# Moving half of the probability transposes that TensorE did to the DMA engines, in a two-head attention loop on one core

## The reference

```
x: (2, 1024, 256)
c_kv = x @ w_dkv                  # rank 64, shared by all heads
c_q  = x @ w_dq                   # rank 192
q, k = heads of c_q, c_kv         # 64 rotary + 128 plain columns each
attn = softmax(q k^T / sqrt(192)) # per head: 1024 queries x 1024 keys
out  = attn v;  y = out @ w_o
x = layernorm(x + y)
x = layernorm(x + (silu(x w1q^T) * (x w3q^T)) w2q^T)
```

## Time and profile before

| | |
|---|---|
| median of three runs | 1011.03 us (1008.86 to 1012.56) |
| the profiled execution | 1020.05 us, of which its span 1017.9 us |
| mean granted clock of TensorE | 0.981 of full speed |
| TensorE busy | 965.2 us, 95% of the span |
| VectorE, ScalarE, GpSimd busy | 741.0, 603.5, 605.3 us |
| one pair of heads, steady | 43.42 us for 16 tiles |

### The profile page before, as it was taken

One profiled execution on the slowest core, in us unless ns is written; L12 is line 12 of the kernel. 1 busy time (PEld: TensorE's weight loads), 2 busy tenths in 40 slices (PEclk: granted clock), 3 DMA queues, 4 the chain that ended last, 5 costly groups with the idle time before them and its releaser, 6 DMA issues.

```text
span 1017.9 us, 18739 instructions
## 1 busy us (share of the span) xinstructions
PE 965.2 (95%) x5622; PEld 696.4 (68%) x5622; DVE 741.0 (73%) x1164; ACT 603.5 (59%) x1036; POOL 605.3 (59%) x643
## 2 busy tenths in 40 slices
PE   7989999999999999998979989999999999997985
PEld 3548766766676766667866866766666676675874
DVE  1756788888888888863456678888888888885455
ACT  2636777777767666751333587766766766764132
POOL 0007777777777777760340787777777777674034
PEclk9799999999999999999989999999999999999998
DMA  9553755545454544566100575655545455457101
GB/s 260 148 217 88 143 103 101 94 95 103 93 96 93 106 94 96 100 140 261 44 23 22 120 129 94 102 100 99 96 89 103 93 97 99 94 103 190 59 1 42
DMA packets 288450, 107.62 MB, mean 106 GB/s; under 512 B 274492, under 2 KB 282512, under 8 KB 287376
## 3 DMA queue, kind: packets, MB, share of 16 engines
q1 hardware_dynamic: 286944, 97.03, 46.1%
q10 hardware_dynamic: 880, 7.86, 2.1%
q0 software_dynamic: 576, 2.10, 0.6%
HBM read 23.85 MB, written 7.60 MB: 31 GB/s over the span
## 4 chain that ended last, share of the span: by engine, by line
PE 73%; issue 10%; DVE 8%; POOL 4%; ACT 2%; DMA 2%; SPq 1%; ACTq 0%; POOLq 0%; DVEq 0%
PE Sa L1045 17%; PE Sb L1045 15%; PE Oa L1072 15%; PE Tb L1054 5%; PE Ta L1054 4%; DVE nmax L753 4%; PE Sb L1096 2%; DVE Q_lo L767 2%; PE Sa L1096 2%; POOL g_lo L415 1%; PE Ob L1082 1%; PE Sb L1172 1%; DMA xr<-in_L_attn_x_dram 1%; POOL P_parts L383 1%; PE Sa L1015 1%
## 5 line engine op out<-in xcount | busy, mean ns | idle before, releaser
L753 DVE TENSOR_REDUCE nmax<-Sa 128x1 f32<-128x1024 f32 x128 | 155.9, 1218 | 78.5 <-PE Sa L1045 77.1
L383 POOL TENSOR_TENSOR P_parts<-probs_a,P_parts 128x512 f16<-128x512 f32 x128 | 169.6, 1325 | 23.5 <-POOL P_parts L380 23.5
L753 DVE TENSOR_REDUCE nmax<-Sb 128x1 f32<-128x1024 f32 x128 | 156.0, 1219 | 20.0 <-PE Sb L1045 20.0
L383 POOL TENSOR_TENSOR P_parts<-probs_b,P_parts 128x512 f16<-128x512 f32 x128 | 149.2, 1166 | 23.9 <-POOL P_parts L380 23.9
L439 ACT ACTIVATE PT_hi<-Ta 128x512 f16<-128x512 f32 x128 | 76.3, 596 | 110.6 <-PE Ta L1054 110.6
L380 POOL TENSOR_SCALAR P_parts<-probs_a 128x512 f16<-128x512 f32 x128 | 80.8, 631 | 75.8 <-ACT probs_a L538 70.4
L380 POOL TENSOR_SCALAR P_parts<-probs_b 128x512 f16<-128x512 f32 x128 | 80.9, 632 | 51.1 <-ACT probs_b L538 48.9
L351 POOL TENSOR_TENSOR turned<-qmul 128x1024 f32<-128x1024 f32 x16 | 38.1, 2404 | 112.2 <-DVE qmul L748 112.2
L1045 PE MATMUL Sb<-K_hi,Q_hi 128*128 128x512 f32 x256 | 91.0, 436 | 7.8 <-ACT probs_b L538 4.0
L1045 PE MATMUL Sa<-K_hi,Q_hi 128*128 128x512 f32 x256 | 93.0, 444 | 0.0
L538 ACT ACTIVATE probs_b<-Sb,nmax 128x1024 f32<-128x1024 f32 x64 | 71.4, 1116 | 33.0 <-DVE nmax L756 33.0
(11 more groups left out here) (298 smaller groups left out, 2118.6 us busy)
## 6 DMA issues: line engine op xcount, KB each, us to landing
QO<-turned SPq DMA_DIRECT2D x64, 128.0 KB, 2.3
TT<-ternary SPq DMA_DIRECT2D x2, 2304.0 KB, 11.5
PT_dma<-P_parts SPq DMA_TRANSPOSE x256, 3.0
ternary<-tern ACTq DMA_DIRECT2D x1, 2304.0 KB, 8.2
wo<-in_L_attn_w_o_dram SPq DMA_DIRECT2D x4, 512.0 KB, 8.1
xq<-in_L_attn_x_dram SPq DMA_DIRECT2D x2, 1024.0 KB, 9.7
wq_high<-Wq_hi ACTq DMA_DIRECT2D x1, 2048.0 KB, 12.7
Wvo_lo<-wvo_low ACTq DMA_DIRECT2D x2, 1024.0 KB, 5.7
```

The costliest lines, as they stand in the source:

```text
L383: nc.gpsimd.tensor_tensor(P_parts[:, n % DEEP, 1, :], src, P_parts[:, n % DEEP, 0, :], ALU.subtract).then_inc(part_lo, 1)
L753: nc.vector.tensor_reduce(nmax[:, n % 4:n % 4 + 1], SS[n % 2][:, :], AX.X, ALU.max, negate=True).then_inc(row_max, 1)
```

## The change

Six of the eight key blocks are turned by DMA in place of four, TensorE turns two. The cast of the high part for DMA goes from GpSimd to ScalarE; GpSimd keeps the subtraction. ScalarE and VectorE evict the turned blocks of two tiles at once, at odd n. The values are multiplied four key blocks at a time, at n = 3, 7, 11 and 15. P_parts grows by half, so a part of Wq_lo is saved to DRAM and read back for the second sequence; buffers in the shared area move.

```diff
-KD = KT // 2
+KP = 2
+KD = KT - KP
+SPILL = 4
...
                 if b + 1 < B:
...
-                    sp.wait_ge(wq_out, 16)
+                    sp.wait_ge(wq_out, 32)
                     sp.dma_start(Wq_hi[...], wq_high).then_inc(wq_in, 16)
+                    sp.dma_start(Wq_lo[:, 0:SPILL]..., wq_low).then_inc(wq_in, 16)
...
# GpSimd
-                    hold(pool, exp_done, EXP0 + tile + 1)
-                    if reused is not None:
-                        hold(pool, part_in[n % DEEP], reused)
-                    nc.gpsimd.tensor_scalar(P_parts[:, n % DEEP, 0, :], src, 1.0, 1.0, ALU.mult,
-                                            ALU.mult).then_inc(part_hi, 1)
                     hold(pool, part_hi, tile + 1)
-                    nc.gpsimd.tensor_tensor(P_parts[:, n % DEEP, 1, :], src, P_parts[:, n % DEEP, 0, :],
+                    nc.gpsimd.tensor_tensor(P_parts[:, n % DEEP, 1, :], probs[n % DEEP][:, KP * P:S],
+                                            P_parts[:, n % DEEP, 0, :], ALU.subtract).then_inc(part_lo, 1)
...
# ScalarE, before the loop over the sequences
             act_.wait_ge(prod_hi, PAIRS)
             act_.wait_ge(qr_hi, 4)
+            act_.wait_ge(prod_lo, PAIRS)
+            act_.wait_ge(qr_lo, 4)
+            act_.dma_start(wq_low, Wq_lo[:, 0:SPILL]...).then_inc(wq_out, 16)
...
+                def part_high(tile, n, reused):
+                    act_.wait_ge(exp_done, EXP0 + tile + 1)
+                    if reused is not None:
+                        act_.wait_ge(part_in[n % DEEP], reused)
+                    copy(P_parts[:, n % DEEP, 0, :], probs[n % DEEP][:, KP * P:S]).then_inc(part_hi, 1)
...
# ScalarE, in iteration n, behind the exponent of tile n+1
-                        if first and n == 1:
-                            act_.wait_ge(wq_out, 16)
+                        if first and n == 0:
+                            act_.wait_ge(wq_out, 32)
+                            act_.wait_ge(rope_sum, b * 2 * GROUPS + 2 * GROUPS)
...
-                        transposed_high(t0 + n, n)
+                        part_high(t0 + n, n, None if first and n < DEEP else 16 * (t0 // DEEP + n // DEEP))
+                        if n % 2:
+                            transposed_high(t0 + n, n)
...
# VectorE, in iteration n, behind the maximum of tile n+2
-                        transposed_low(t0 + n, n)
+                        if n % 2:
+                            transposed_low(pair * (TILES // 2) + n // 2, n)
...
# TensorE
-                    for k in range(KD):
+                    for k in range(KP):
...
-                            if n % 2 == 1:
-                                for k in range(n % 8 - 1, n % 8 + 1):
+                            if n % 4 == 3:
+                                for k in range(n % 8 - 3, n % 8 + 1):
                                     values(pair * 2 + n // 8 - 1, 1 - n // 8, k)
```

More of the change, by code:

```diff
@@ L62, in build @@
     wq_high = nc.dram_tensor("wq_high", [P, H * 2 * P], F, kind="Internal").ap()
+    wq_low = nc.dram_tensor("wq_low", [P, SPILL * 2 * P], F, kind="Internal").ap()
     wvo_low = nc.dram_tensor("wvo_low", [P, PAIRS * D], F, kind="Internal").ap()
@@ L116, in build @@
         (TT,), _ = lay(HEAD_AT, ("TT", [P, W], R))
-        (PT_hi, PT_lo, PT_dma), _ = lay(
-            SHARED_AT, ("PT_hi", [P, 2, 2, KD, HALF], F16), ("PT_lo", [P, 2, 2, KD, HALF], F16),
-            ("PT_dma", [P, 2, 2, 2 * KD, HALF], F16))
+        (PT_dma, PT_hi, PT_lo), _ = lay(
+            SHARED_AT, ("PT_dma", [P, 2, 2, 2 * KD, HALF], F16), ("PT_hi", [P, 2, 2, KP, HALF], F16),
+            ("PT_lo", [P, 2, 2, KP, HALF], F16))
+        PT_END = SHARED_AT + 2 * 2 * 2 * KD * HALF * 2
         (xq, xT, tcos, tsin, wkr, wkv, wdq, wdq_b), WORK_AT = lay(
@@ L132, in build @@
         (turned,), _ = lay(SHARED_AT, ("turned", [P, 2, S], F))
-        PT_BYTES = KT * S * 2
         (res1,), AT = lay(WORK_AT, ("res1", [P, 4, D], F))
-        assert AT <= SHARED_AT + 2 * PT_BYTES
-        (xr, res0, x1a), _ = lay(
-            SHARED_AT + 3 * PT_BYTES, ("xr", [P, QT, D], F), ("res0", [P, 4, D], F), ("x1a", [P, 4, D], F))
+        assert PT_END - 24 * S <= WORK_AT and AT <= PT_END - 16 * S
+        (res0, xr, x1a), AT = lay(
+            PT_END - 16 * S, ("res0", [P, 4, D], F), ("xr", [P, QT, D], F), ("x1a", [P, 4, D], F))
+        assert AT <= PT_END
         (x1b, x1T_hi0, x1T_lo0), AT = lay(
-            SHARED_AT + 2 * PT_BYTES, ("x1b", [P, 4, D], F), ("x1T_hi0", [P, KC, HALF], R),
-            ("x1T_lo0", [P, KC, HALF], R))
-        assert AT <= SHARED_AT + 3 * PT_BYTES
+            PT_END, ("x1b", [P, 4, D], F), ("x1T_hi0", [P, KC, HALF], R), ("x1T_lo0", [P, KC, HALF], R))
+        assert AT <= SHARED_AT + 64 * S
         def tok(halves, t):
@@ L289, in _ @@
                 if b:
-                    sp.wait_ge(wq_in, 16)
+                    sp.wait_ge(wq_in, 32)
                     sp.sem_inc(wq_ready, 1)
@@ L389, in pair_pool @@
                         h = n // 8
-                        split_probs(pair * TILES + n, n,
-                                    None if first and n < DEEP else 16 * (pair * TILES // DEEP + n // DEEP))
+                        low_probs(pair * TILES + n, n)
                         if n % 8 == 0 and not (first and h == 0):
@@ L1047, in scores, with transpose_probs @@
                     last.then_inc(scores_ready, 1)
-                def transpose_probs(tile, n, waited):
+                def transpose_probs(tile, tile2, n, waited):
                     if not waited:
                         pe.wait_ge(exp_done, EXP0 + tile + 1)
-                    pe.wait_ge(pt_lo, tile + 1)
-                    for k in range(KD):
-                        last = nc.tensor.transpose(TS[n % 2][:, k * P:(k + 1) * P],
+                    if n % 2 == 0:
+                        pe.wait_ge(pt_lo, tile2 + 1)
+                    for k in range(KP):
+                        at = (n % 2 * KP + k) * P
+                        last = nc.tensor.transpose(TS[n // 2 % 2][:, at:at + P],
                                                    probs[n % DEEP][:, k * P:(k + 1) * P], ident[:, :])
@@ L1133, in pair_pe @@
                             scores(t0 + n + 2, (n + 2) % TILES, pair + (n + 2) // TILES)
-                        transpose_probs(t0 + n, n, not (last and n >= TILES - 2))
+                        transpose_probs(t0 + n, pair * (TILES // 2) + n // 2, n, not (last and n >= TILES - 2))
                         if first and n == 8:
```

38 lines of the change are left out of this document (20 added, 18 removed).

## The result

The changed kernel takes 1059.59 us (median of four runs, 1058.29 to 1063.81), the kernel before 1011.79 (four runs, one more than the three behind 1011.03): a ratio of 1.0476, with a 95% interval of 1.0426 to 1.0526. Slower, as forecast, inside the range of 1020 to 1068, and 17 us above the 1043 that was named. The two profiled executions are 1058.37 and 1020.05 us, 38 us apart, the medians 48: the profiled execution of before was some 9 us above its own median, that of after was not.

The account below looks back on a forecast made before the run. PE bounds the kernel, 5.27 us per two tiles, just above a 4.40 us loop of scores, maximum and exponent. Terms of 16.1 us a sequence, twice, plus 0.4, say 32, added to the median 1011.03 gave 1043; range 1020 to 1068.

Parts of the forecast that it names:

- The turn and the cycle: Attention loop: scores, maximum, exponent, next scores into the same banks take at least 4.40 us; four tiles take 11.24 us.
- S4: Third scores after a block of values: wait for an exponent, cannot start before 4.40 us after the first scores.
- S5: Fourth scores after a block of values: start at 6.71 us, not 6.03, since cast and eviction delay their exponent on ACT.
- the block of 24: The 24 value matmuls on PE after every fourth tile: 2.72 us.
- the cast's hold: Time the new 768 column cast holds ACT's queue ahead of an exponent: 0.72 us, between 0.49 and 0.95.
- the 13 us more: Whole time added if the cast on ACT cost the skill's 0.94 us, holding ACT 0.22 us longer.
- the rest of a pair: Beyond four cycles of 11.24 us, the Q_lo split at n = 12 delays an exponent some 0.2 us: pair 45.2 us.
- The ends: Outside the steady pairs, per sequence: tiles without values 0.5 + 0.4 us more, last pair 1.2, tail up to xr 2.7.
- (a): Rival: PE is the only bound, 1.2 us per four tiles come out, 70 us off, 941 us; chance 0.04.
- (b): Rival: the cast hardly holds ACT, cycle 10.56 us, 1003 us; chance 0.09, including a cast near its lower bound.
- (c): Rival: DMA sets the pace, ACT waits at its cast for landings; 400 us more, milder case 1100; chance 0.05.
- (d): Rival: PE's clock falls because PE waits more; 1057 us if tiles without values ran at half clock; chance 0.06.

Follow-up runs that it names:

- the last one: Changed kernel with values two key blocks at a time, both casts behind the next even tile's exponent, Q_lo splits at n = 11 and 15: 994.50 us, ratio 0.9758.

## Why the prediction was right, and where its sum was off

**The turn and the cycle.** Right, with its mechanism, and to the hundredth: 11.24 us predicted, 11.25 measured. S4 at 4.43 (4.40 predicted), S5 at 6.74 (6.71), the block of 24 at 2.71 (2.72), the cast's hold at 0.73 (0.72). The gaps on PE are those foretold, 0.91 ahead of S4 and 0.41 ahead of S5. ACT's busy time is the one sign that was off: 36.8 us of a pair, not 39, since I had added recorded times, which overlap. With the cast out of the way the cycle is the 10.56 that the prediction named. The Trainium skill (ScalarE: Activation LUTs, Rules for kernel authors) gives the 0.94 us for an ACTIVATE whose bias is a pointer operand, which this cast does not have; the trace shows a recorded 0.84 and a hold of 0.73, so the 13 us more did not come. For an operation that follows another one of ACT the distance between starts is the price. The 0.72 was a halfway guess between two rows; the copies of 512, 768 and 1024 columns hold ACT for 0.48, 0.73 and 0.95 us, so the guess was near because the price goes nearly with the columns.

**Which of the two matters more.** The grouping by four. The prediction said that gathering the blocks leaves one of two turns bare and eats the whole saving on PE; the run with nothing but the grouping shows 2.6 us a pair lost where PE's work is unchanged. The cast's place adds 0.7 in a cycle without other waits, and 0.9 in a pair as it stands.

**The step that was mis-sized: the rest of a pair.** The prediction charged DVE's queue with 0.2 us a pair ("the Q_lo split at n = 12 now comes between maxima 2 and 3"). It measured 1.3. Three things were missing: that the scores of the next queries read what the split writes (PE's 1.27 us wait is for Q_lo); the split at n = 15, behind which the normalising and the reciprocal stand ahead of the maximum; and that the splits grow, from 1.21 to 1.31 us in the kernel before to 1.43 to 1.78. The run with the splits moved has a pair of 45.17 and so shows that this is the place.

**The ends.** Without values, scores into the same banks start at 115.83, 120.22, 124.62 and 129.11: turns of 4.39, 4.40 and 4.49, where 4.5 was said. I take the first sequence apart by the starts of DVE's reciprocals and by PE's final values, which start at 490.44 against 471.46: 19.0 us later, 16.1 predicted. The first scores start at 103.46 against 104.86. The six middle pairs lie between the reciprocals at 152.41 and 430.18 (152.53 and 412.97 before), the second of them in DVE's timeline:

```profile
430.18 0.18 DVE L789 RECIPROCAL rden<-den 128x8 f32<-128x8 f32 x1
```

| term, one sequence | predicted | measured |
|---|---|---|
| up to the first scores, and the tiles without values | +0.9 | 103.46 against 104.86, then 25.14 against 24.80: -1.1 |
| the half pair | +0.85 | 23.81 against 22.87: +0.9 |
| six pairs | +10.5 | 277.77 against 260.44: +17.3 |
| from there to the final values (last pair and tail) | +3.9 | 60.26 against 58.49: +1.8 |
| sum | 16.1 | 19.0 |

The tail was right up to the load: xr goes out 476.63 - 462.33 = 14.3 us after the scores that count as 0 (13.2 to 15.9 predicted, 11.8 before). It gives 0.9 back at once, since the load then takes 5.87 us where it took 6.73, and 1.35 in the products between the load and the final values, before and after:

```profile
464.36 7.10 PE Sb L1172 x48
```

```profile
484.69 5.75 PE Sb L1185 x48
```

The same 48 matmuls ran at a granted clock of 0.79 before and 1.00 after. That makes up the 2.1 by which this row came out lower. In the second sequence they took 6.17 and 5.99 us, and this term is 61.7 against 58.0: +3.7, near the 3.9 predicted. After both sequences the final values are 38.7 us later. So the terms fell short by 6 us (33 against 38.7: 14 too little for the pairs, 8 too much for the ends), and the other 10 of the 17 are the step "I add the 32 to the median": the profiled execution of before stood 9 us above its median, and that distance belonged to it. A good part of it goes with the clock: the executions of the kernel before took 1008.6 to 1010.8 us at a mean granted clock of 0.989 and 1018.3 to 1022.7 at 0.976 to 0.979, and the profiled one had 0.981. Beside the 1.35 us above, its stretch from the final values of the first sequence to the first scores of the second took 112.89 us against 110.24, with windows at 0.67, 0.72 and 0.60 (from 510, 530 and 535, 5 us each) where the changed kernel has one at 0.66. Why the clock differs from execution to execution is open. So of the 8 us too much for the ends some 4 are before's slower profile; with these set aside the terms fell short by about 10 us and not 6, and it was luck that the ends hid a part of what the pairs lacked.

**GpSimd and DMA.** The subtraction takes 1.65 us (1.8 taken) and is hidden: POOL waits for ACT's cast, for up to 2.3 us. The transposes, against the earlier trace rows:

```profile
L310 SPq DMA_TRANSPOSE PT_dma<-P_parts x256: 1273/1430/3212, 114.1 to 972.2; - x128
...
DMA to landing us min/median/max: 3.6/3.7/6.2
```

Half as many blocks again cost 0.2 us of issue and 0.7 of landing, less than the 0.6 and 1.5 allowed for.

**The rivals.** (a) PE the only bound: out, PE stands for 5.9 us a pair. The Trainium skill (Perfetto Trace Analysis, Identifying the Most-Contended Engine) would have the busiest engine relieved first; for TensorE it reads the headroom from the useful work and the weight loads, and not from the matmul time, and the weight loads are busy for 68% here, VectorE for 73%. Relieved TensorE was, by 47 us, and the time rose. With the order around it mended, the same relief ends 2.4% below the kernel before; the moved splits alone end 0.7% below it without any relief. (b) The cast hardly holding ACT: out, 0.73 us. (c) DMA as the pace: out, the median landing is 3.7 us. (d) The clock: not in the pairs of the changed kernel (1.00; 0.982 in the mean of the execution), but real one step further: two of the experiments lost to it. At the end of the first sequence's attention it did fall, to 0.50 from 469 to 475, behind waits of PE of 0.99 and 1.81 us that ended at 466.76 and 469.00. It cost little there: the chain from 465.8 to 482.5 runs through ACT, GpSimd, SP and the load of xr, and not through PE.

## What to carry to other kernels

Where an engine at 95% sits just above a latency loop (here 5.27 us of PE against a turn of 4.40 through maximum and exponent), its filler work is cover: spread it so that every turn keeps some. Gathered into every second turn it left the loop bare here and cost more than the work saved. Before an operation is moved to an engine with idle time, write down that engine's order at the operation that ends the loop: ahead of it the cast cost its hold in each cycle (0.69 of 0.73 us), behind it almost nothing, as long as no rare operation was late in the same cycle. When slack shrinks, walk through the rare operations too (here two splits a pair): what 0.87 us of slack hid costs 1.1 to 1.6 us a pair without it.

## What the hardware showed that I had not expected

VectorE and GpSimd take turns in some of their operations. The Q_lo split (DVE, two operands in SBUF) takes 1.22 us alone, but 1.43, 1.68, 1.78 and 2.00 where GpSimd's subtraction had begun before it. In the changed kernel and in the last one:

```profile
334.30 1.65 POOL L381 TENSOR_TENSOR P_parts<-probs_b,P_parts 128x768 f16<-128x768 f32 x1 [1.12 <-ACT P_parts L434]
335.25 1.78 DVE L777 TENSOR_TENSOR Q_lo<-QO,Q_hi 128x1024 fp32r<-128x1024 f32 x1
```

```profile
232.01 1.65 POOL L381 TENSOR_TENSOR P_parts<-probs_b,P_parts 128x768 f16<-128x768 f32 x1
232.73 2.00 DVE L778 TENSOR_TENSOR Q_lo<-QO,Q_hi 128x1024 fp32r<-128x1024 f32 x1
```

The subtraction had 0.70 and 0.93 us to go, and the split is 0.56 and 0.78 longer than alone: each time all of the rest but some 0.15. Where the split begins first, it keeps its 1.22 us and the subtraction pays (2.44 us in place of 1.65, in the kernel with values by two and the splits moved, with the split 0.31 us ahead). The kernel before shows it as well (a subtraction of 2.18 us in place of 1.17 behind a split that began 0.06 us earlier). The cast on VectorE, with one operand in SBUF, does the same: 0.56 us alone, 1.00 where the subtraction had 240.66 + 1.65 - 241.73 = 0.58 us to go. The row maxima, which read PSUM, keep their 1.22 us beside the same subtraction. The Trainium skill (SBUF — State Buffer, SBUF: two separate sides) states this as an exclusive lock, held for a whole instruction, between GpSimd and a VectorE operation with two SBUF inputs; the trace agrees to within those 0.15 us. With it the prediction could have foreseen the 0.2 to 0.6 us by which the two splits of a pair grew.

The clock's price is uneven: the same wait of PE of 1.9 us was followed by a stretch at half clock in two of three neighbouring pairs and by none in the third, some 2.2 us apart; the changed kernel's waits of 1.27 and 1.69 us in its pairs, and the 1.98 us with one cast later and the splits moved, were followed by none in the pairs looked at. What decides it was not tried.
